# A graph layer's front rebuilt as three blocks, with segment maxima kept per edge lane

## The reference

```python
xn = layernorm(x)
h = xn @ W.T;  e_src = h @ a_src;  e_dst = h @ a_dst      # graph attention
e = leaky(e_src[src] + e_dst[dst], 0.2)                   # edges and self loops
m = segment_max(e, dst);  e = exp(e - m[dst]);  s = segment_sum(e, dst)
out = segment_sum(e / s[dst] * h[src], dst) + bias
gnn = xn + elu(out)
q, k, v = relu(xn @ Wq.T), relu(xn @ Wk.T), xn @ Wv.T     # linear attention, 8 heads
mix = (q @ (k.T @ v) * temperature / clip(q @ sum(k), 100)) @ Wproj.T + bproj
x = x + gnn + mix
x = x + moe_ffn(layernorm(x))                             # 8 experts, top 2
```

## Time and profile before

| | us |
|---|---|
| median of 3 runs | 4465.39 |
| lowest, highest | 4462.83, 4474.2 |
| the profiled execution, its own time | 4469.66 |
| its span, first to last instruction | 4467.9 |

### The profile page before, as it was taken

How to read it: one execution, slowest core, us unless ns; L and a number is a source line. 1 busy time by engine, 2 the same in 40 slices (tenths; PEclk the granted TensorE clock), 3 DMA queues, 4 the chain that set the end, 5 groups by cost and what they waited for, 6 DMA issues and landing times. The chain is left out here.

```text
span 4467.9 us, 74456 instructions
## 1 busy us (share of the span) xinstructions
PE 3297.3 (74%) x11832; PEld 1901.1 (43%) x11833; DVE 2373.8 (53%) x6284; ACT 1297.3 (29%) x3555; POOL 1768.2 (40%) x1993
## 2 busy tenths in 40 slices
PE   4777799999999002777777878888887689999700
PEld 2333699866666001222333333333333355555400
DVE  2333466555555444444555555555556557777733
ACT  0111244311111001544454444444445112222100
POOL 1222344200000001666565555555555136666554
PEclk9888655699999556999998999999999679999955
DMA  3222222366666565665565656555555512222277
GB/s 137 92 93 93 73 77 77 93 155 149 148 142 146 130 133 118 183 184 176 167 191 167 183 164 179 173 176 175 170 182 172 198 43 92 92 92 92 89 233 227
DMA packets 379008, 631.60 MB, mean 141 GB/s; under 512 B 43319, under 2 KB 219610, under 8 KB 377699
## 3 DMA queue, kind: packets, MB, share of 16 engines
q0 software_dynamic: 93472, 318.59, 23.6%
q1 hardware_dynamic: 271395, 287.00, 23.3%
q10 hardware_dynamic: 14112, 25.70, 1.5%
HBM read 538.06 MB, written 93.06 MB: 141 GB/s over the span
## 5 line engine op out<-in xcount | busy, mean ns | idle before, releaser
L975 PE MATMUL acc_ps<-rows,W 128*128 128x512 f32 x1908 | 1041.5, 674 | 348.3 <-DVE W L1079 221.3
L858 POOL DMA_INDIRECT rows<-h_rows,idx x954 | 955.0, 1001 | 737.2 <-PE acc_ps L975 468.9
L975 PEld LDWEIGHTS acc_ps<-rows,W 128*128 128x128 f32 x1908 | 360.1, 209 | 1003.6 <-issue 837.8
L899 ACT ACTIVATE e_pos<-pqb,es_col 128x128 f32<-128x128 f32 x954 | 372.7, 391 | 148.2 <-DVE e_top L1073 131.7
L641 DVE SCALAR_TENSOR_TENSOR masked<-pair,cst 128x192 f32<-128x192 f32 x636 | 250.1, 416 | 309.0 <-DMA pair<-pair_rows 241.4
L1073 DVE TENSOR_TENSOR e_top<-e_pos,e_neg 128x384 f32<-128x384 f32 x318 | 169.8, 558 | 420.0 <-ACT e_neg L900 343.0
L900 ACT ACTIVATE e_neg<-pqb,es_col 128x128 f32<-128x128 f32 x954 | 367.8, 386 | 0.0
L553 PE MATMUL row_ps<-es_lut,hot 49*128 49x128 f32 x1632 | 348.5, 418 | 18.9 <-POOL hot L543 18.9
L553 PEld LDWEIGHTS row_ps<-es_lut,hot 49*128 49x128 f32 x1632 | 348.2, 330 | 19.1 <-issue 19.1
L847 POOL MEMSET zb<- 1x512 bf16 x1 | 0.5, 515 | 890.1 <-POOLq L741 890.1
L1079 DVE SCALAR_TENSOR_TENSOR W<-window,dst_col,e_top 128x128 f32<-128x128 f32 x954 | 275.8, 346 | 60.3 <-PE acc_ps L975 59.3
(11 more groups left out here) (255 smaller groups left out, 4883.8 us busy)
## 6 DMA issues: line engine op xcount, KB each, us to landing
pair<-pair_rows SPq DMA_DIRECT2D x636, 192.0 KB, 4.2
y_rows<-y SPq DMA_DIRECT2D x105, 256.0 KB, 2.0
hi_row<-src_hi SPq DMA_DIRECT2D x204, 128.0 KB, 2.8
rows<-h_rows,idx POOLq DMA_INDIRECT x954, 3.8
xb<-in_x SPq DMA_DIRECT2D x49, 256.0 KB, 2.7
h_rows<-hb ACTq DMA_DIRECT2D x49, 256.0 KB, 2.1
res_rows<-xrest SPq DMA_DIRECT2D x49, 256.0 KB, 2.2
a_own<-h_rows SPq DMA_DIRECT2D x49, 256.0 KB, 2.7
```

Source lines behind the costliest of these rows:

```text
L858: nc.gpsimd.indirect_dma_start(G[j][:], None, h_rows, bass.IndirectOffsetOnAxis(ap=idx[:, j:j + 1], axis=0)).then_inc(row_in[j], 16)
L899: nc.scalar.activation(e_pos[:, half, j, :], pqb[s][:, 0, :], ACT.Exp, bias=es_col[:, ds(at_tile + (half * HT + j), 1)])
L975: nc.tensor.matmul(acc_ps[s][:], W[:, j, :], G[j][:], start=False, stop=False, skip_group_check=True).then_inc(row_used, 1)
```

## The change

The three stretches before the aggregation are written anew.

1. **Layer norm alone** (lines 344 to 438 of the changed kernel): `xb`, `xn` and the PSUM tiles have four buffers. A tile of `h` is not made here. PE does four transposes and the four two-column `e_ps` matmuls, ACT copies to `hxnT`, `qT`, `es_n` and `ed_n`, and DVE keeps scale and shift of each row (`ln_keep`). `h_rows` and `res_rows` are not written in this block.
2. **Lookup and h** (440 to 581): 102 lookups of 1024 edges in 51 rounds of two, with the h matmuls of one node tile between the two. The *low* seven bits of src are spread in bf16 over 128 partitions (`lo_row`, 256 KB), the one-hot has 128 rows in bf16, and e_src is split into three bf16 parts (`es_part`) of 49 columns each, so a lookup is 24 short matmuls. DVE makes a mask of the high part (`mask`, two SBUF inputs), multiplies with PSUM (`prod`) and sums (8 x 49 to 8). `hi_col` holds the edge's value less the lowest afterwards. No edge value goes to memory.
3. **Peak and q, k, v** (600 to 800): the q, k, v chain is as before. The maximum is kept as `top`, 128 edge lanes by 6 x 128 nodes: for each edge tile one two-scalar operation (equal to the destination, times the value) over 128 columns, then a maximum of 384 columns twice a visit. `top` is folded once per node tile to `by_node` and the 49 tiles are turned on PE at the end (`turn_ps`). GpSimd makes the residual from a second load of x and `ln_keep`, and clears `top`. SP loads x and stores `res_rows` in this block.
4. `wproj` is loaded in the fold block, which waits for it, and not in the setup.

```diff
-                sp.dma_start(pair_rows[0].rearrange("(p c) -> p c", p=ROWP), lin_d[:]).then_inc(saved, 16)
-                sp.dma_start(src_hi.rearrange("(p c) -> p c", p=ROWP), lin_f[:]).then_inc(saved, 16)
+                sp.dma_start(src_lo.rearrange("(p c) -> p c", p=ROWP), lin_lo[:]).then_inc(saved, 16)
...
+    # layer norm block, PE
+                            for c in range(KC):
+                                last = nc.tensor.transpose(T_ps[s][:, c * P:(c + 1) * P], xn[s][:, c * P:(c + 1) * P], C["ident"])
+                            for c in range(KC):
+                                last = nc.tensor.matmul(e_ps[s][:, 0:2], hT[s % 2][:, c, :], u[:, c, :], start=(c == 0), stop=(c == KC - 1))
...
+    # lookup block, PE
+                            for j in range(LT):
+                                for k in range(3):
+                                    last = nc.tensor.matmul(row_ps[b][:, j * NT:(j + 1) * NT], hot[b][:, j * P:(j + 1) * P], es_part[:, k, :],
+                                                            start=(k == 0), stop=(k == 2))
+                            lookup(2 * j, 0, hot_ready, j + 1)
+                            if has_node:
+                                for c in range(KC):
+                                    last = nc.tensor.matmul(h_ps[s][:], hT[s][:, c, :], wg[:, c, :], start=(c == 0), stop=(c == KC - 1))
+                            lookup(2 * j + 1, 1, hot_odd, j + 1)
+    # lookup block, GpSimd and ACT
+                            nc.gpsimd.tensor_scalar(hot[0][:], lo_row[2 * s][:], C["iota_col"], None, ALU.is_equal).then_inc(hot_ready, 1)
+                            nc.scalar.activation(hot[1][:], lo_row[2 * s + 1][:], ACT.Abs, bias=C["minus_col"]).then_inc(apart, 1)
+                            nc.scalar.activation(hot[1][:], hot[1][:], ACT.Relu, bias=C["ones"], scale=-1.0).then_inc(hot_odd, 1)
...
-                                    nc.vector.scalar_tensor_tensor(masked[:, h * QE:(h + 1) * QE], pair[h][:, 0, :], C["node_id"][:, ds(t, 1)],
-                                                                   pair[h][:, 1, :], ALU.is_equal, ALU.mult).then_inc(rows_used, 1)
-                                nc.vector.tensor_reduce(top[:, 1:2], masked[:], AX.X, ALU.max).then_inc(pk_step, 1)
-                                nc.vector.tensor_tensor(top[:, 0:1], top[:, 0:1], top[:, 1:2], ALU.max).then_inc(pk_step, 1)
+                                for h in (0, 1):
+                                    for j in range(h * HT, h * HT + HT):
+                                        put = nc.vector.tensor_scalar(masked[:, j, :], window[:], dst_col[:, ds(at_tile + j, 1)], hi_col[:, ds(at_tile + j, 1)],
+                                                                       ALU.is_equal, ALU.mult)
+                                for h in (0, 1):
+                                    nc.vector.tensor_tensor(top[s][:, low_half(h), :], top[s][:, low_half(h), :], masked[:, low_half(h), :], ALU.max).then_inc(topped, 1)
+    # peak block, GpSimd, per node tile
+                            nc.gpsimd.tensor_scalar(rest[s][:], rest[s][:], ln_now[:, 0:1], ln_now[:, 1:2], ALU.mult, ALU.add).then_inc(rest_step, 1)
+                            nc.gpsimd.tensor_tensor(rest[s][:], rest[s][:], pbias[:], ALU.add).then_inc(rest_ready, 1)
+                                hold(pool, fold_step, 3 * t + 1)
+                                nc.gpsimd.memset(top[s][:], 0.0).then_inc(top_clear, 1)
```

More of the change, by code:

```diff
@@ L57 @@
 RT = ET // ROWP
-TB = ET // 8
+LT = 8
+LC = ET // LT
+assert LC % 2 == 0 and NT <= LC and LT * NT <= D
 VISIT = 65536 // VT + 1
@@ L328, in gps_layer @@
             with pj:
[L329 to L334, removed]
-                sd = [sb(pj, f"sd{s}", [P, 2]) for s in (0, 1)]
-                rest = [sb(pj, f"xrest{s}", [P, D]) for s in (0, 1)]
@@ new lines, in _, with fetch @@
+                    @block.scalar
+                    def _(act):
+                        def fetch(t, s):
+                            hold(act, h_done, t + 1)
+                            nc.scalar.copy(hT[s][:], qT[:, :, ds(t * P, P)]).then_inc(fetched, 1)
+                        act.sem_inc(h_done, 2)
+                        fetch(0, 0)
+                        for j, s, i, has_node in rounds(act):
+                            act.wait_ge(rows_done, 2 * j + 2)
+                            act.wait_ge(lo_in[2 * s + 1], 16 * i + 16)
+                            nc.scalar.activation(hot[1][:], lo_row[2 * s + 1][:], ACT.Abs, bias=C["minus_col"]).then_inc(apart, 1)
+                            if not isinstance(j, int) or j < NT - 1:
+                                fetch(j + 1, 1 - s)
+                            act.wait_ge(apart, j + 1)
+                            nc.scalar.activation(hot[1][:], hot[1][:], ACT.Relu, bias=C["ones"], scale=-1.0).then_inc(hot_odd, 1)
@@ new lines, in _, with low_half @@
+                        nc.vector.tensor_scalar(above[:], es_n[:], lows[:, 0:1], None, ALU.add).then_inc(fin, 1)
+                        def low_half(h):
+                            return slice(h * HT, (h + 1) * HT)
+                        for t, s, i in tiles(dve):
+                            first, limit, shift = visit_range(dve, t)
+                            if not isinstance(t, int) or t > 0:
+                                hold(dve, fold_step, 3 * t)
+                            nc.vector.tensor_scalar(window[:], C["iota_row"], C["tile_start"][:, ds(t, 1)], None, ALU.add).then_inc(win_ready, 1)
+                            hold(dve, win_ready, t + 1)
+                            hold(dve, top_clear, t + 1)
@@ L736, in _ @@
                         nc.tensor.transpose(pq_ps[0:NT, P:2 * P], pq[:, 1, :], C["ident"]).then_inc(pq_ready, 1)
+            with ExitStack() as fo:
+                abT = sb(fo, "abT", [P, KC, P])
+                ks_sb = sb(fo, "ks_sb", [P, KC])
+                wproj = sb(fo, "wproj", [P, KC, D])
+                fold_ps = [psum(fo, f"fold_ps{c}") for c in range(KC)]
                 fold_dve, fold_pe = sem("fold_dve"), sem("fold_pe")
                 with nc.Block() as block:
+                    @block.sync
+                    def _(sp):
+                        sp.dma_start(wproj[:], a["wproj"]).then_inc(wproj_in, 16)
                     @block.vector
```

567 lines of the change are left out of this document (294 added, 273 removed).

## The result

The changed kernel takes 3848.51 us (median of 4, 3837.19 to 3856.01) where the kernel before takes 4465.02 beside it: ratio 0.8614, 95% interval 0.8589 to 0.8638. The profiled execution took 3856.01, its span is 3854.2. The prediction was 4046, range 3915 to 4210: the direction was right, the time lies 198 us under the forecast and 66 under the range.

A forecast was written before the change was run, and what follows sets the result against it. Bounds taken: PE's chain of waits in the front, half-clock PE in the lookups, DMA of broadcast pairs in the peak block. Aggregation starts at 1329.7, not 1749.2: 4467.9 - 419.5 = 4048.4, median 4046 us; range 3915 to 4210.

The forecast's parts named there:

- Setup, layer norm block: Setup 4 us shorter; then a layer norm block bound by PE at half clock, 2.65 us per tile, ending at 186.5.
- I take 7.1 us: Lookup and h block: length of one round, 6.3 us at full clock plus stretching; 49 rounds make 348 us.
- I take 0.06: Lookup rounds: price in us of one short bf16 matmul with 49 moving columns, so 24 cost 1.44 us.
- two things stretch it: Lookup rounds: clock of 0.85 to 1, and GpSimd's one-hot meeting DVE's masks, lengthen the round from 6.3 to 7.1 us.
- From below 6.0 per round: Lookup and h block: lower bound of the round, against 12.0 from above; block 326 to 620 us.
- Peak block: DVE bounds it: 159 visits at 2.7 us, 4.7 per tile besides, 64 for GpSimd, 4 more; sum 727 us.
- the meeting: Peak block: GpSimd's operations and DVE's hold each other up, 1.3 us per tile, 64 us in all.
- The rule weighed against the sum: Lookup rounds: a skill rule of 81 ns per load-and-matmul pair would make each round 1.0 us longer, the sum 49.
- Rival 1: Every GpSimd operation meets DVE in full: peak block +122 us, rounds +25, total 4193; chance 0.17.
- Rival 2: Peak block falls to PE's floor, visits at 2.4, and rounds at 6.3: -97 and -39 us, total 3910; chance 0.11.
- Rival 3: PE stays at half clock through the lookup rounds: round 12.0 us, +240, total 4286; chance 0.07.
- rival 4: Lookup rounds: a short matmul costs the old 0.213 us at half clock, round 17.1, +501, total 4547; chance 0.03.

The follow-up runs named there:

- x1: The changed kernel with every burst of 24 short matmuls issued four times over in place; 4262.57 us.
- x5: The changed kernel with a GpSimd addition of 1024 float32 scrap columns put ahead of each one-hot; 4170.58 us.
- x3: The changed kernel without GpSimd's scaling and bias addition for the residual in the peak block, so the residual is wrong; 4039.45 us.
- x13: The changed kernel unaltered, run again on another chip; 3844.04 us, ratio to the kernel before 0.8614.
- x2: The changed kernel with f32 one-hots and e_src not split, 8 f32 matmuls for each 24 bf16 ones; 4193.26 us.

## Why the prediction was right in direction and wrong in size

- **Setup, layer norm block.** Right in mechanism: PE is the busiest, at the half pace, 2.45 a tile for 2.65. The 0.20 is that I added the scores at their full length of 1.71, whose tail overlaps the next operation, and a gap of 0.06: start to start the transposes take 0.89 and the scores 1.56, without a gap. -11 us.
- **Lookup round, the failed step.** Two terms of "I take 7.1 us" fell. The short matmul, "I take 0.06", is 0.026 (x1: 0.025): -1.6 us a round. And "two things stretch it", 0.8 us, did not happen: the clock stayed at 1.00 from 198.1 us on, and the masks pass the one-hot (x5 shows that an addition in its place would have stopped them). Together 2.45, of which h (3.52 from start to start for 3.43) and gaps give 0.2 back: the round is 2.24 shorter. The range failed here too. "From below 6.0 per round" left the short matmul no room under 0.06, though the earlier trace rows had a row for it: h's 512 columns take 0.43 a record, so 49 columns 0.04. That end was not used, and even it is above the 0.026 measured. The rounds make 49 x 2.24 = 110 of the stage's -113 us.
- **Peak block.** A visit is 2.56 for 2.7: -22 us over 159. The rest of a tile, without the meeting, is (626.5 - 159 x 2.56)/49 = 4.48, from x3's length of the block (444.0 to 1070.5), which holds the fixed 4 us too; the forecast had 49 x 4.7 + 4: -15. The meeting was put at 1.3 a tile, 64 us, and costs 29 (x3): -35. Sum -72 for -71.2. The meeting is smaller because the six compares and the maxima hardly meet GpSimd: it begins its turn behind the fold, and is done at 706.31 where the first compare starts at 707.24.
- **Turn step, fold.** 11.1 and 17.6 for 15 and 18.2. The fold waits for wproj, as forecast, though 7.4 us and not 5:

```profile
1099.74 7.21 PE L794 MATMUL turn_ps<-cst,by_node 128*128 128x128 f32 x32 [52.33 <-DVE by_node L701]
...
1121.11 6.36 PE L830 MATMUL fold_ps<-wproj,abT 128*128 128x512 f32 x8 [7.38 <-DMA wproj<-in_wproj]
```

- **The rest.** Taken as unchanged; 7.1 us longer in this pair of executions. That is within what one kernel varies by: in x13, the same kernel, the aggregation starts at 1126.8 of 3840.8 us, so the rest takes 2714.0, 12 us less than here and 5 less than before.
- **The rivals.** Rival 1 (every GpSimd operation meets DVE in full) is refuted by x3 and by the one-hot's rows. Rival 2 had the right direction, 3910, at 0.11, and was still 62 us too long, for the same 6.3 per round; its first term is also mis-added, since from 727 to PE's floor of 615 are 112 us and not 97. Rival 3 (half pace in the rounds) and rival 4 (0.213 per short matmul) are refuted by x1. What they rest on, the pace of the old lookups, was measured without a wide matmul among them.
- **The rule weighed against the sum.** The burst of 48 loads and matmuls took 1.23 us. The 81 ns a pair that the Trainium skill (TensorE: Matmul & The Clock Gate, section Back-to-back issue gap) gives for 128 columns would have made it 3.9 us, by my estimate (48 x 0.081). The burst moves 49 columns, and no run here had such a stream of 128 in bf16, so the figure itself isn't tested; the measurement decides for this burst.

So where do the 614 us of the spans come from? Front and lookups went from 802.8 to 393.7: the f32 lookups at the half pace, 348 us of PE, became 48 x 0.026 x 51 = 64, of which x2 puts 118 us down to bf16; and h, which in the front stood beside a chain of waits in a tile of 8.6 us, now fills the round. The peak block with the turn went from 877.8 to 666.9, as DVE no longer waits for broadcast pairs: 241 us of DVE's idle time stood at `pair` before, and after it no wait of DVE in this block is for a DMA. These shares are read from the rows; of the three rebuilt stages the experiments tested single terms, and none put an old stage back.

## What to carry to other kernels

Price the part that repeats most often from both sides, and look for the row that bounds it from below as carefully as for the one above: 2448 cheap matmuls at 0.026 and not 0.06 are about 84 of the 194 us that the forecast was off. Try to merge a stage of small matmuls with one of wide ones: here the wide ones brought the whole to PE's full pace, and even a useless one paid (2.18 for 2.45 us a tile), while a second one cost more than it gave (3.02). Where DVE waits, for GpSimd or for a result of its own, put the wait into time in which DVE reads registers, ahead of the read and not behind it.
